# A mixture-of-experts tile loop: SiLU begun on the gate half, TensorE's table reads moved behind the transpositions, four tiles a turn

## The reference

```python
scores = softmax(xt @ Wr); topk_w, topk_idx = top_k(scores, 2); topk_w /= topk_w.sum(-1)
g = silu(einsum('th,ehd->etd', xt, Wg)); u = einsum('th,ehd->etd', xt, Wu)
out_all = einsum('etd,edh->eth', g * u, Wd)             # 8 experts, 256 -> 512 -> 256
out = sum(gathered(out_all) * topk_w) + silu(x @ Sg) * (x @ Su) @ Sd
```

## Time and profile before

| | us |
|---|---|
| median of 3 runs | 1096.64 |
| lowest and highest | 1096.44, 1098.18 |
| the profiled execution, its own time | 1101.61 |
| its span | 1099.7 |
| PE busy in the span | 1032.2 (94%) |

### The profile page before, as it was taken

One profiled execution on the slowest core, in us unless ns is written; L12 is line 12 of the kernel. 1 busy time (PEld: TensorE's weight loads), 2 busy tenths in 40 slices (PEclk: granted clock), 3 DMA queues, 4 the chain that ended last, 5 costly groups with the idle time before them and its releaser, 6 DMA issues.

```text
span 1099.7 us, 19315 instructions
## 1 busy us (share of the span) xinstructions
PE 1032.2 (94%) x5960; PEld 901.9 (82%) x5961; DVE 764.7 (70%) x1290; ACT 489.6 (45%) x914; POOL 442.0 (40%) x445
## 2 busy tenths in 40 slices
PE   6898997799999999999999999989999999999994
PEld 5676776799999998999988787878888888888883
DVE  7988998899999987787878343333444444347886
ACT  6745755774344444666751222222322222233326
POOL 1000201555544446322100787975633200018886
PEclk9999998999999999999999999999999999999997
DMA  8100000010000000311250557464413111213335
GB/s 315 70 32 20 1 29 1 1 35 1 0 0 0 0 1 1 120 40 39 64 205 6 187 172 242 141 183 160 156 52 107 56 48 54 70 58 108 123 106 191
DMA packets 41350, 87.83 MB, mean 80 GB/s; under 512 B 5970, under 2 KB 27732, under 8 KB 39892
## 3 DMA queue, kind: packets, MB, share of 16 engines
q0 software_dynamic: 9696, 35.66, 10.5%
q1 hardware_dynamic: 20804, 39.20, 10.0%
q10 hardware_dynamic: 10800, 12.32, 3.6%
HBM read 57.80 MB, written 29.36 MB: 79 GB/s over the span
## 4 chain that ended last, share of the span: by engine, by line
PE 53%; DVE 19%; DVEq 10%; POOL 8%; issue 5%; ACT 4%; DMA 1%; ACTq 0%; POOLq 0%
PE PS L1857 14%; PE PS L1859 13%; PE PS L1858 13%; POOL gathered L1043 6%; PE PS L2260 3%; PE PS L2012 2%; DVEq L1433 2%; DVEq L1280 2%; POOL pause L1047 1%; DVEq L1447 1%; PE PS L2244 1%; DVE hx L1292 1%; PE PS L1910 1%; DVEq L1293 1%; DVE qinv L1283 1%
## 5 line engine op out<-in xcount | busy, mean ns | idle before, releaser
L1794 DVE TENSOR_TENSOR hb<-PS,gs 128x512 f32<-128x512 f32 x71 | 49.1, 692 | 154.0 <-ACT gs L784 143.4
L1043 POOL DMA_INDIRECT gathered<-expert_outputs,pos x64 | 66.7, 1043 | 139.5 <-DMA expert_outputs<-ye 127.2
L1857 PE MATMUL PS<-EWs,xeh 128*128 x284 | 119.8, 422 | 0.0
L784 ACT ACTIVATE gs<-PS 128x512 f32<-128x512 f32 x71 | 42.5, 598 | 162.3 <-PE PS L1859 154.0
L1859 PE MATMUL PS<-EWs,xel 128*128 x284 | 112.5, 396 | 0.0
L1858 PE MATMUL PS<-EWs,xeh 128*128 x284 | 111.8, 394 | 0.0
L1857 PE MATMUL PS<-WGh,bxh 128*128 128x352 f32 x256 | 88.0, 344 | 13.4 <-DVE hv L1427 10.5
L2012 PE MATMUL PS<-WD,htf 128*128 128x256 f32 x384 | 88.5, 380 | 1.6 <-ACT htf L573 1.5
L1857 PE MATMUL PS<-EWs,heh 128*128 x284 | 85.7, 302 | 3.9 <-issue 3.9
L789 ACT ACTIVATE heh<-PS 128x512 fp32r<-128x512 f32 x71 | 42.5, 598 | 104.4 <-PE PS L2260 86.9
L1798 DVE TENSOR_TENSOR hel<-PS,heh 128x512 fp32r<-128x512 f32 x71 | 49.1, 691 | 55.0 <-ACT heh L789 46.3
(11 more groups left out here) (387 smaller groups left out, 3013.5 us busy)
## 6 DMA issues: line engine op xcount, KB each, us to landing
raw_of<-experts POOLq DMA_DIRECT2D x6, 1536.0 KB
expert_outputs<-ye SPq DMA_DIRECT2D x71, 128.0 KB
xe<-tokens_by_expert ACTq DMA_DIRECT2D x65, 128.0 KB
xraw<-xT SPq DMA_DIRECT2D x8, 512.0 KB, 4.1
X<-x SPq DMA_DIRECT2D x1, 4096.0 KB, 13.3
tokens<-X SPq DMA_DIRECT2D x8, 512.0 KB, 3.1
y<-X SPq DMA_DIRECT2D x7, 512.0 KB
raw_of<-experts SPq DMA_DIRECT2D x2, 1536.0 KB, 9.5
```

Of the source, the lines that this page charges most:

```text
L784: act.activation(gs[:, h], PS[:, 2], ACT.Silu).then_inc(e_si, 1)
L1043: pool.indirect_dma_start(out=gathered[c][:, j, t], out_offset=None, in_=YS, in_offset=bass.IndirectOffsetOnAxis(ap=pos[:, j, 4 * c + t:4 ...
L1794: dve.tensor_tensor(hb[:, h], PS[:, 3], gs[:, h], ALU.mult).then_inc(e_hb, 1)
L1857: pe.matmul(out_, wh, vh, start=first, stop=False)
```

## The change

`e_gu` is raised twice a tile, once after each half. ACT's SiLU waits for the first, DVE's product for the second as well. In PE's `tile` the transpositions of `hb` come before `place_of(i)`; where the place of tile i-1 must be read anew, that is done just before the down matmuls. PE's loop has four tiles a turn (15 turns, tiles 5 to 64) and six tiles are written out behind it. Inside a turn only the first tile reads the former place anew.

```diff
             def x_high_e(i, h):
-                wait(act, e_gu, i - 1)
+                wait(act, e_gu, 2 * i - 2)
             def silu_e(i, h):
-                act.wait_ge(e_gu, i + 1)
+                act.wait_ge(e_gu, 2 * i + 1)
             def hidden_e(i, h):
+                dve.wait_ge(e_gu, 2 * i + 2)
                 dve.wait_ge(e_si, i + 1)
...
                 for w in range(2):
                     for k in range(KD): ...
-                mm.then_inc(e_gu, 1)
+                    mm.then_inc(e_gu, 1)
...
             def tile(i, h, before=None, first=False, final=False):
+                if not first:
+                    h_transpose_e(i - 1, 1 - h)
                 place = place_of(i)
                 expert, at = place % E, place // E * SLOT
-                if not first:
-                    if before is None:
-                        before = place_of(i - 1)
-                        before = before // E * SLOT
-                    h_transpose_e(i - 1, 1 - h)
                 pe.wait_ge(w_ready, expert + 1)
                 gate_up_e(i, h, at)
                 if not final:
                     x_transpose_e(i + 1, 1 - h)
                 if not first:
+                    if before is None:
+                        before = place_of(i - 1)
+                        before = before // E * SLOT
                     down_e(i - 1, 1 - h, before)
                 return at
...
-            with pe.Fori(2, (NE - 5) // 2) as r:
-                at = tile(2 * r + 1, 1)
-                tile(2 * r + 2, 0, at)
-            at = tile(NE - 4, 1)
-            for i in range(NE - 3, NE):
+            with pe.Fori(0, (NE - 7) // 4 - 1) as r:
+                at = tile(4 * r + 5, 1)
+                for i in range(6, 9):
+                    at = tile(4 * r + i, i % 2, at)
+            at = tile(NE - 6, 1)
+            for i in range(NE - 5, NE):
                 at = tile(i, i % 2, at, final=i == NE - 1)
```

## The result

The changed kernel takes 1100.98 us (median of 9 runs, 1099.10 to 1102.69) where the kernel before, on the same chip, takes 1096.69 (9 runs, 1096.32 to 1099.36): 1.0033 of the time, with a 95% interval of 1.0022 to 1.0044. It is slower by 4.3 us; 3.6 were forecast. The two profiled executions differ by only 1.0 (spans 1099.7 and 1100.8), because the first 24 tiles, which hold waits for rows, came out 1.8 shorter in the second.

The account below looks back on a forecast made before the run. PE, timed from T0 (start of a tile's last gate-and-up matmul), was taken to bound the kernel: 20 tiles of 5.07 and 20 of 5.23 give +3.8, with the tail +3.6, 1100.2 us; range 1092.5 to 1103.

Parts of the forecast that it names:

- SiLU on the gate half: ACT and DVE: product starts at T0 + 0.43 instead of +1.06; the new wait costs 0.04 in even, 0.20 in odd tiles.
- rival 1: DVE: the product's wait costs 0.04 in all tiles, 5.07 each in the loop, +0.5, 1097.1 us; chance 24%.
- The read behind `hb`: PE: the 0.75 read joins the stretch behind `hb`; gate and up start at T0 + 2.43 in even, 2.59 in odd tiles.
- rival 2: PE: sequencer goes on past the pending wait, or the read is cheaper; in full 4.83 a tile, 1087.7 us; chance 19%.
- The wait's rule: PE's sequencer: a matrix instruction with a pending wait holds up the register work behind it until `hb` is there.
- Rival 3: PE: the transpositions' wait is looked at only when the array arrives, T0 + 1.80; 5.72 a tile, 1123 us; 4% with rival 4.
- Turn-opening tiles: PE, a turn's first tile: saved address (0.10) and ALU_OP before the transpositions were put against each other, no extra time.
- The last six tiles: Tiles written out behind tile 64: gate and up at T0 + 2.33 as today; one turn less gives back 0.16.
- The first 24 tiles: Stretch up to 744 us: PE's changes are absorbed by waits for rows; put at 0, bounds 0 and +1.5.
- Four tiles a turn: PE's loop: fewer branches are worth nothing, since the branch is over before `hb` comes; no fetch stall.
- Rival 4: PE's loop: a code fetch at each turn, up to 14 x 5.75 = 80 us; 4% together with rival 3.

Follow-up runs that it names:

- e5: The changed kernel with the two waits of DVE's product swapped, `e_si` first and the new one on `e_gu` last: 1100.28 us, 1.0004 of the kernel before.
- e8: The changed kernel with the table read done twice behind the transpositions: 1146.54 us, 1.0433 of the kernel before.
- e1: The changed kernel with the tile's own read put back ahead of the transpositions: 1078.51 us, 0.9911 of the kernel before; repeated, 1077.87 us, 0.9914.
- e3: The kernel before with only the new read order (own read behind the transpositions, former place before the down matmuls): 1137.67 us, 1.0455 of the kernel before.
- e7: The changed kernel with PE's loop of two tiles a turn as before: 1098.41 us, 1.0095 of the kernel before.
- edit 2: The part of the change that moves both place reads, own behind the transpositions, former before the down matmuls; alone in the kernel before: 1137.67 us, 1.0455.
- e2: The kernel before with the early SiLU alone (two increments of `e_gu`): 1085.58 us, 0.9979 of the kernel before.

## Why the prediction was right, step by step

- **SiLU on the gate half.** SiLU at T0 - 0.93 to -0.96 in all but one of the 40 tiles (-0.86 in the first tile of ACT's turn), `hb` at T0 + 0.43 and + 0.59: as forecast (-0.9, 0.43, 0.6). The ALU_OP at 902.1 and e5 show the 0.16 as the price of the wait's place; rival 1 (0.04 in all tiles) is e5, another kernel.
- **The read behind `hb`.** Gate and up at T0 + 2.43 in even and 2.59 in odd tiles: as forecast. e8 measures a read there at 0.63, against 0.65 for a read without the address, so rival 2 falls. e1 shows the counterpart, tile by tile the 4.82 to 4.83 that rival 2 gave.
- **The wait's rule.** The load comes about 0.10 after the release, at T0 + 1.28, and 0.48 before the weight load of the transpositions at T0 + 1.76. So a pending wait holds register work only until its semaphore is there and not until the array gets to the instruction. Rival 3 (1123) falls. By the Trainium skill (Perfetto Trace Analysis, Tensor Engine Instruction) the sequencer is ready for its next instruction once it has pushed one into the wait queue. The trace agrees as far as this: once the wait is over the sequencer goes on, although the array is still busy. It doesn't agree for a wait that is pending: there the read stood until `hb` came.
- **Turn-opening tiles, mis-sized.** "I put both against each other", the address saved (0.10) against the ALU_OP. Nothing was saved. The register work of the read (shortest, median, longest of two), first behind the T0 of tile 54, then behind that of tile 56 (906.87), where tile 57 opens a turn:

```profile
L2273 PEldq FUSED_REGOPS  x2: 42/96/151, 897.7 to 898.2; - x2
```

```profile
L2273 PEldq FUSED_REGOPS  x2: 42/100/157, 908.1 to 908.6; - x2
L2273 PEldq TENSOR_LOAD <-of_tile x1: 304/304/304, 908.2 to 908.2; - x1
```

  The address instruction of 42 ns is in both, and the ALU_OP comes on top: the load starts at T0 + 1.38 instead of +1.28, gate and up at 2.55 on average instead of 2.43. A tile that opens a turn takes 5.18 where 5.07 was forecast; 10 tiles of 0.11 are +1.1, the difference between the measured 4.86 and the forecast 3.8.
- **The last six tiles, mis-sized.** -0.16 was forecast, -0.60 measured. Gate and up start at T0 + 2.22 there instead of 2.33 in most of them; the read starts at the release (T0 + 1.18) and takes about 0.64, as forecast; the rest behind it takes 0.40 and not the 0.50 of the loop.
- **The first 24 tiles.** Put at 0 with bounds 0 and +1.5; the two pairs of profiles gave -1.8 and +1.2. Waits for rows cover them there. e3 shows the end of that cover: on a chip where the kernel before takes 1088, its first 24 tiles take 17 to 19 us more than those of the other kernels. The forecast was for the chip of the profile; the bound isn't good for every chip. On the fourth chip the changed kernel would by the estimate above be 8 to 9 us slower, where the range of the forecast ends at 6.4. That the result was measured on a chip whose early tiles wait for rows is a piece of luck.
- **Four tiles a turn.** Nothing in the changed kernel beyond what e7 shows, 1.6 to 1.9 us in 40 tiles. That is 10 turn openings fewer of 0.11, and a late table load (one tile of 5.64 in e7): so not quite the nothing that I forecast, which rested on the mis-sized turn-opening tile. No fetch shows: the 14 taken branches last 0.22 each, as before, and the next register instruction follows each after 0.06 or 0.10, as before. Rival 4 falls. PE's branch over the whole loop of the changed kernel:

```profile
L2313 PEldq COMPARE_BRANCH  x15: 79/222/235, 651.0 to 948.0; - x15
```

The sum came out well because these errors offset each other: +1.1 in the 40 tiles, -0.4 in the tail. The 4.86 and the -0.60 make 4.3, which is the measured difference; it leaves nothing for the first 24 tiles, and the two pairs of profiles can't tell that to better than 1.5. The mechanism and the even and odd tiles were right on their own.

The experiments point to a better kernel, run twice: the early SiLU with the read left ahead of the transpositions, 0.9911 and 0.9914 of before, and 0.9921 with the loop of two tiles as before. The gain of SiLU (0.63 of a wait) and the loss by the moved read (0.63 to 0.75) had cancelled in the even tiles; the former place read at the down matmuls is the part of edit 2 that is worth keeping.

## What to carry to other kernels

Register work behind an engine instruction that waits is not free: in this kernel it stood until the semaphore came, and a read there cost 0.63 us a tile. So put table reads and address work ahead of the wait they can hide under, and behind it only what has cover after it. Two edits of one stage are to be summed as a new stage, not as two differences: here -2.4 and -4.0 and +49.7 alone became +4.3 together (on another chip), and the change with the tile's own read left ahead of the wait gave -9.5. When a tile's time differs by its place in the loop, read each place by itself, since the tile bound by another engine and the tile bound by its own sequencer answer to different edits.

## What the runs showed that I hadn't expected

- Where a wait stands among several of one instruction is worth 0.16 us in DVE's odd tiles, the first of its turns: 0.59 with the new wait first (and the computed value behind it), 0.43 with it last (e5), 3.9 us for the kernel in all.
- An earlier `hb` made turn-opening tiles longer, 5.25 for 5.12 (e2): the sequencer is released by `hel`, which hardly moved, and not by the array, so it is later relative to an array that got faster.
- Chips differ more than this change: the kernel before takes 1087.5 and 1088.0 on two of them and 1096.7 and 1099.5 on two others. In the profiles of the slower two the first 24 tiles take 132 to 134 us in the kernels before and changed, with two to four tiles of 6 to 12 us (tile 23 of the changed kernel takes 9.97); on the faster two the kernels without a read behind `hb` take 120.3 to 122.8, with at most one such tile. Up to tile 0 (608 to 610 us) and behind tile 70 (123.1 to 124.1 us) the profiles of all four hardly differ, so the chips differ in the waits of the first 24 tiles.
